# The seam of a first FFN and an attention: batch 0's output and norm into the last FFN units, batch 1's end, norm, keys and values into the first three head pairs

## What is computed

```python
x = x + 0.5 * ffn(layernorm(x))      # "first FFN"
x = x + attn(layernorm(x))
x = x + 0.5 * ffn(layernorm(x))      # same weights, "second FFN"

def ffn(h):       # 4 experts mixed per batch by a gate on the pooled tokens
    w = top-2 gate of relu(mean(h) @ Wg1 + bg1) @ Wg2 + bg2
    q, k, v = h @ (sum_e w_e W_e) + b          # 16 heads of 8
    out = softmax(q k^T / sqrt(8)) v
    return out @ Wo + bo

def attn(h):      # 16 query heads of 64, one key/value head, a null key
    q = h @ Wq / 8; kv = concat(null_kv, h @ Wkv)
    out = causal softmax(q kv^T) kv
    return out @ Wout
```

## Time and profile before

| | us |
|---|---|
| three runs, median (lowest to highest) | 1282.89 (1278.74 to 1284.65) |
| the profiled execution, own time | 1280.69 |
| its span | 1279.0 |
| busy in the span: PE, DVE, ACT, POOL | 1157.0, 1061.4, 941.1, 307.7 |
| end of the first FFN's last value products | 378.57 |
| first score tile of the attention | 399.83 |
| first maximum of pairs 0, 1, 2, 3 | 401.66, 437.00, 465.26, 493.26 |

### The profile page before, as it was taken

One profiled execution on the slowest core, in us unless ns is written; L12 is line 12 of the kernel. 1 busy time (PEld: TensorE's weight loads), 2 busy tenths in 40 slices (PEclk: granted clock), 3 DMA queues, 4 the chain that ended last, 5 costly groups with the idle time before them and its releaser, 6 DMA issues. The chain is left out here.

```text
span 1279.0 us, 31986 instructions
## 1 busy us (share of the span) xinstructions
PE 1157.0 (90%) x10884; PEld 502.0 (39%) x10884; DVE 1061.4 (83%) x1787; ACT 941.1 (74%) x2001; POOL 307.7 (24%) x535
## 2 busy tenths in 40 slices
PE   4499999998987899999999999998769999999996
PEld 3122222222225555555566565555522222222223
DVE  6899999998987777777755777776589999998997
ACT  3179999998983677777755777775339999998994
POOL 4400000022000354444432444443330000000200
PEclk9689999999997999999999999998869999999998
DMA  4812212354210001000000000000431212244422
GB/s 109 247 32 56 64 52 60 81 88 85 66 41 19 18 23 29 18 17 18 18 18 18 18 18 18 18 18 2 149 99 48 69 47 55 75 79 88 83 48 67
DMA packets 51793, 69.55 MB, mean 54 GB/s; under 512 B 21168, under 2 KB 29296, under 8 KB 51696
## 3 DMA queue, kind: packets, MB, share of 16 engines
q1 hardware_dynamic: 51696, 68.26, 21.7%
HBM read 37.30 MB, written 22.54 MB: 47 GB/s over the span
## 5 line engine op out<-in xcount | busy, mean ns | idle before, releaser
L959 DVE TENSOR_REDUCE neg_max<-ps 128x1 f32<-128x1024 f32 x512 | 594.5, 1213 | 26.6 <-PE ps L1230 22.8
L795 ACT ACTIVATE arena<-ps 128x512 f32<-128x512 f32 x1024 | 545.3, 597 | 84.2 <-PE ps L1245 71.9
L1261 PE MATMUL ps<-arena 128*32 128x256 f32 (+1 forms) x3584 | 317.1, 426 | 25.0 <-ACT arena L795 24.2
L1245 PE MATMUL ps<-arena 50*128 50x512 bf16 x1024 | 309.2, 388 | 6.2 <-DMA arena<-max_dram 5.6
L1230 PE MATMUL ps<-arena 48*128 48x512 bf16 x1024 | 282.6, 397 | 16.8 <-DVE neg_max L959 14.4
L1031 DVE TENSOR_REDUCE a_neg_max<-ps 128x1 f32<-128x129 f32 (+7 forms) x256 | 191.9, 750 | 110.4 <-PE ps L1382 109.4
L634 POOL TENSOR_SCALAR arena<-arena,a_rsum 128x128 f32<-128x128 f32 (+7 forms) x256 | 191.1, 747 | 310.8 <-DVE a_rsum L1050 303.5
L731 ACT ACTIVATE arena<-ps,a_neg_max 128x129 f32<-128x129 f32 (+7 forms) x256 | 189.2, 739 | 51.0 <-DVE a_neg_max L1031 38.5
L1377 PE MATMUL ps<-arena 64*128 64x128 f32 (+6 forms) x512 | 192.6, 457 | 0.0
L1375 PE MATMUL ps<-arena 64*128 64x321 f32 (+7 forms) x512 | 187.9, 450 | 4.9 <-DVE neg_s_null L1062 1.9
L1245 PEld LDWEIGHTS ps<-arena 50*128 50x128 bf16 x1024 | 71.7, 94 | 258.2 <-ACT arena L795 226.3
(11 more groups left out here) (125 smaller groups left out, 820.5 us busy)
## 6 DMA issues: line engine op xcount, KB each, us to landing
arena<-stack_dram SPq DMA_DIRECT2D x128, 192.0 KB, 3.4
stack_dram<-arena SPq DMA_DIRECT2D x48, 256.0 KB, 3.8
o_dram<-arena SPq DMA_DIRECT2D x32, 256.0 KB, 2.1
arena<-arena SPq DMA_DIRECT2D x32, 256.0 KB, 3.6
arena<-o_dram SPq DMA_DIRECT2D x30, 256.0 KB, 4.4
arena<-max_dram SPq DMA_DIRECT2D x256, 1.0 KB
x<-in_L_attn_x SPq DMA_DIRECT2D x2, 512.0 KB, 4.9
max_dram<-max_T SPq DMA_DIRECT2D x64, 8.0 KB, 1.7
```

The source lines that it names most:

```text
L795: nc.scalar.activation(probs[:, t, :], ps[:, EXP_BANK[t], :], ACT.Exp, scale=F_SCALE).then_inc(probs_ready, 1)
L959: nc.vector.tensor_reduce(neg_max[:, g, t:t + 1], ps[:, bank:bank + 2, :].rearrange("p a b -> p (a b)"), AX, ALU.max, negate=True).then_in ...
L1245: ins = nc.tensor.matmul(ps[:, bank, :], stack[rows, g, 1, kt * P:(kt + 1) * P], stack[rows, g, 0, h * HALF:(h + 1) * HALF], start=True, s ...
L1261: ins = nc.tensor.matmul(ps[row:row + 32, PV_BANK, cols], v_unit[:, g, t // 2, :], probs[:, t, cols], start=j == 0 and c0 == 0 and g % 2 == 0,
```

## The change

- Batch 0's product with Wo (`finish_0_half`) goes into the last two units: its halves ahead of score tiles (g, kt) = (2, 6) and (3, 1) of the last iteration, through banks 3 and 4. DVE's `finish` of batch 0 and its norm follow at once; ACT's square root stands after the exponential t = 8 of the last unit.
- POOL adds 0.5 * bo to all of x in the seventh of eight iterations of each FFN (`bias`), so `finish` needs one instruction for each half.
- `null_values` goes to the start of the first FFN, between the max tiles of unit 0 and those of unit 1; ACT copies it out after its splits.
- After the last unit PE has only the transposes, queries, keys, values and null scores of batch 0.
- Batch 1's sums, reciprocals and scaling are shared out: additions and scaling on POOL, `recip_1` on DVE (first half before the attention, second half in steps 1 and 3), `normalize_last` in step 6. Its products with Wo are four takes "Z" in steps 8 to 14 of pair 0, added by DVE's `add_quarter`.
- Batch 1's norm is in pair 1 (one `bn_stats` in each of steps 0 to 7, square root at ACT's step 9, reciprocal in step 11, the rest in steps 12 to 15); its transposes, keys, values and null scores are takes "N", "K", "A", "S" in steps 1, 2, 4, 6, 8, 10 of pair 2.
- PE's wait for batch 1's values is dropped from pairs 0 to 7.

```diff
+        SECOND_STEPS = {t: ("Z", t // 2 - 4, 0) for t in (8, 10, 12, 14)}
+        for t, take in ((1, ("N", 0, 0)), (2, ("N", 1, 0)), (4, ("K", 0, 0)), (6, ("K", 1, 0)), (8, ("A", 0, 0)), (10, ("S", 0, 0))):
+            SECOND_STEPS[2 * NS + t] = take
...
+                def bias():
...
+                    for b in range(B):
+                        pool.wait_ge(xn_ready, 4 * B * ph + 2 * b + 2)
+                        for g in range(2):
+                            xs = x[:, b * NT + 4 * g:b * NT + 4 * g + 4, :]
+                            nc.gpsimd.tensor_tensor(xs, xs, bo[:, :].unsqueeze(1).broadcast_to([P, 4, C]), ALU.add).then_inc(x_biased, 1)
...
+                if ph == 0:
+                    pool.wait_ge(o_loaded[1], 16 * (PAIRS_B - 1))
+                    r = slice(0, P - LR)
+                    for g in range(2):
+                        s = slice(g * HALF, (g + 1) * HALF)
+                        for kind, total in ((1, den), (0, num)):
+                            nc.gpsimd.tensor_tensor(total[r, 1, s], o_all[r, 1, 2 * g, kind, :], o_all[r, 1, 2 * g + 1, kind, :],
+                                                    ALU.add).then_inc(den1_ready, 1)
+                    pool.wait_ge(den1_ready, 4)
...
             def attention():
+                scale_1(0)
                 for t in range(NS):
                     normalize(0, t)
...
+                    if t == 5:
+                        scale_1(1)
...
+                    if s == 3:
+                        act.wait_ge(o_stored[1], 16 * (UNITS // NB) + 16)
+                    if s == NS + 9:
                         norm_std(B + 1, 1)
...
+                    if t == 8 and g == 3 and isinstance(it, int) and it == UNITS // NB - 1:
+                        norm_std(B, 0)
...
-                    nc.vector.tensor_tensor(ytmp[:, :, :].rearrange("p (a t) c -> p a t c", a=2), y,
-                                            bo[:, :].unsqueeze(1).unsqueeze(1).broadcast_to([P, 2, 2, C]),
-                                            ALU.add).then_inc(dve_link, 1)
...
+                nc.vector.scalar_tensor_tensor(xs, y, 0.5, xs, ALU.mult, ALU.add).then_inc(x_ready, 1)
...
+                    if s in (1, 3):
+                        recip_1(1, (s - 1) // 2 * (HALF // 2), (s + 1) // 2 * (HALF // 2))
+                    if s == 6:
+                        normalize_last(0)
...
+                    if 0 <= t < NT:
...
+                        ins = nc.vector.bn_stats(stats[:, NT + t, :], x[:, NT + t, :])
...
+                    if t == 11:
+                        dve.wait_ge(std_ready, B + 2)
+                        dve.wait_ge(xT_done, 2 * B + 2)
+                        link(nc.vector.reciprocal(rstd[:, NT:2 * NT], rstd[:, NT:2 * NT]))
...
+                    if isinstance(it, int) and it == UNITS // NB - 1 and (g, kt) in ((2, 6), (3, 1)):
+                        finish_0_half(0, g - 2)
                     score_tile(g, it, kt, 0)
...
+                for k in range(2):
+                    cols, tok = slice(k * C, (k + 1) * C), slice((2 * z + k) * P, (2 * z + k + 1) * P)
+                    nc.tensor.matmul(ps[:, bank, cols], num[0:P - LR, 1, tok], wo[0:P - LR, :], start=True, stop=False)
+                    ins = nc.tensor.matmul(ps[:, bank, cols], num_last[r, k * P:(k + 1) * P], wo_last[r, :], start=False, stop=True)
...
+                if ph == 0:
+                    null_values()
                 for t in range(NT):
                     max_tile(1, i0, t)
+                if ph == 0:
+                    pe.wait_ge(null_ready, 1)
```

More of the change, by code:

```diff
@@ L619, in body @@
                             null_weights()
+                        if isinstance(ul, int) and ul == (HB + 1) * NB and g == 2:
+                            bias()
                 body(0, False)
@@ L646, in attention @@
             def attention():
+                scale_1(0)
                 for t in range(NS):
                     normalize(0, t)
[L649 to L653, removed]
+                    if t == 5:
+                        scale_1(1)
+                for pg in range(1, 4):
+                    for t in range(NS):
+                        normalize(pg, t)
+                        if t in (1, 5) and pg % 2:
+                            add_null(pg // 2, t // 4)
+                with pool.Fori(4, B * PAIRS) as i:
                     for t in range(NS):
@@ L1150, in ffn @@
                     recip_0(ph, g)
-                for g in range(2):
-                    normalize_1(ph, g)
-                finish(ph * B, 0)
                 if ph == 0:
+                    finish(0, 0)
                     norm(B, 0)
-                normalize_last(ph)
-                if ph == 0:
+                    recip_1(0, 0, HALF)
                     for h in range(2):
@@ L1163, in ffn @@
                     values_in(0)
-                finish(ph * B + 1, 1)
+                    null_scores_in(0, Q_BANK)
+                else:
+                    for g in range(2):
+                        normalize_1(ph, g)
+                    finish(ph * B, 0)
+                    normalize_last(ph)
+                    finish(ph * B + 1, 1)
             ffn(0)
@@ L1310, in keys, with second_take @@
+            def second_take(kind, k):
+                if kind == "Z":
+                    out_take(k)
+                    return
+                wait_taken((kind, k, 0))
+                if kind == "N":
+                    norm_T_half(B + 1, k, TAKE_BANK["N", k, 0])
+                elif kind == "K":
+                    keys(1, k)
+                elif kind == "A":
+                    key_values(1)
+                else:
+                    null_scores(1, TAKE_BANK["S", 0, 0])
             def keys(b, h):
@@ L1549, in ffn @@
                     key_values(0)
-                finish_last(ph)
+                    pe.wait_ge(w_null_ready, 7)
+                    pe.wait_ge(probs_ready, TB + TB * UNITS)
+                    null_scores(0, Q_BANK)
+                else:
+                    finish_0(ph)
+                    finish_1(ph)
+                    finish_last(ph)
             ffn(0)
```

218 lines of the change are left out of this document (126 added, 92 removed).

## The result

| | before | after |
|---|---|---|
| median of 20 runs, us | 1282.17 | 1291.87 |
| lowest to highest | 1278.27 to 1285.92 | 1278.74 to 1297.91 |
| profiled execution, own time and span | 1280.69, 1279.0 | 1289.16, 1287.4 |
| ratio after / before, 95% interval | | 1.0058 (1.0038 to 1.0077) |

The change makes the kernel slower by 0.6%, where 2.6 us of gain were forecast; the median lies above the forecast range, which ended at 1288.0. The spread says more than the median: the runs of before lie within 8 us; those of after are in two groups, nine from 1278.7 to 1289.2 and eleven from 1291.7 to 1297.9. They go with the mean granted clock: the five quickest have 0.959 to 0.962, the eleven slowest 0.942 to 0.951.

The account below looks back on a forecast made before the run. PE bounds full pairs (27.38 of 28.00 us); the seam is a 21.3 us chain with little throughput work. Terms sum to -2.6 us, 1278.1 from the profiled 1280.7; with the median 2.2 higher, 1280.3 us; range 1272.5 to 1288.0.

Parts of the forecast that it names:

- Pair 0: First attention pair: root, null-score wait and value product leave, other work enters; 4.6 us shorter, 5.3 gained with first maximum.
- the takes Z: Batch 1's output products in pair 0: 3.75 us of PE at the lower clock, mostly in waits; 1.1 us lost.
- The clock: Last unit: the pause for the root may lower PE's clock; 1.0 us lost, between 0 and 4.0.
- B: Rival: moved work is paid again in full in pairs 1 and 2; total +5.2 us, 1288.1 us; chance 0.15.
- C: Rival: the clock falls in the last unit and stays down; 3.0 us more, 1283.3 us; chance 0.11.
- three signs of being wrong: Pair 0 stays at 35 us, pair 1 exceeds 33, or the last unit grows by more than 6 us.
- the null product: Start of the first FFN, between two max tiles: delays DVE's next maximum; 2.6 us lost, bounds 1.1 and 3.4.
- the chain from the values to the first score: Seam: batch 0's finish and norm leave it; values end at 383.0, first score at 392.5 instead of 399.8.
- pair 2: Third attention pair: batch 1's transposes, keys, values and null scores at PE's bound; 5.1 us lost, bounds 4 and 8.3.
- the inserted halves: Last unit: two insertions of batch 0's product on PE, 0.75 us each; 1.5 lost, bounds 0 and 2.1.
- the root with its clock: Last unit: ACT's root with two table loads, 2.9 us in full, and 1.0 for a fall of the clock.
- Pair 1: Second attention pair: DVE's added pieces cost 0.8 us, ACT's root 2.1; 2.7 lost, bounds 1 and 7.3.

Follow-up runs that it names:

- run 1: The changed kernel measured once more with no edit: median 1284.05 us, ratio 1.0039 to the kernel before.
- run 10: The changed kernel without the 16-row products of batch 1's output, two 112-row products a take: median 1282.46 us, ratio 0.9999 to the kernel before.
- run 5: The changed kernel with both moved norms' roots on DVE (linear guess, three Newton steps) instead of ACT: median 1285.08 us, ratio 1.0029 to the kernel before.
- run 8: Only the change's part inside the first FFN, roots on DVE, null product at the seam: median 1274.17 us, ratio 0.9951 to the kernel before.
- run 7: The changed kernel with output takes grouped, null product back at the seam, roots on DVE: median 1280.42 us, ratio 0.9990 to the kernel before.

## Why the prediction was wrong, point by point

| | forecast, us | first profile | run 1's profile |
|---|---|---|---|
| start of the first FFN | +2.6 | +2.8 | +2.8 |
| last unit, with the clock | +5.4 | +6.7 | +6.7 |
| values' end to first score | -11.7 | -12.1 | -11.9 |
| first score to first maximum | -0.7 | -1.2 | -1.2 |
| pair 0 | -4.6 | +7.6 | -2.4 |
| pair 1 | +2.7 | +4.1 | +4.2 |
| pair 2 | +5.1 | +5.4 | +5.5 |
| end of the attention (two levels) | 0 | -4.3 | -4.3 |
| end of the second FFN | -1.4 | -1.7 | -2.2 |
| all the rest | 0 | +1.1 | +2.6 |
| span | -2.6 | +8.4 | -0.2 |

The last column is no sign that the change costs nothing: at the level that the kernel before had at the end of the attention, the quick execution would be 4 us slower than it, and the first profile 13.

**The step that failed is "Pair 0"**, and in it the term of the takes Z: 3.75 us of PE at the lower clock, counted 1.1 on the path. That row had eight 112-row products in a line, and I left out the eight 16-row products that the takes also have, and the turns. The eight alone would have been 1.26 us by the row of `finish_last`; among the 112-row ones they cost as much as these. Measured, a take is 2.9 us at the lower level and 1.67 at the full one: 11.6 or 6.7 us. A block of 2.9 us inside a loop of two us a step isn't hidden by its waits. With half of the products gone (run 10) pair 0 is 31.1 us.

**The deeper fault is in "The clock".** I priced a fall of the clock in the last unit, at 1.0 us within 0 and 4.0, and none in pair 0, although before the clock was also down for a good part of it. It is this level that decides 10 us: 43.0 against 33.0 us of pair 0 in the same kernel. So no rival had the time of the measured median: B, the slowdown, gives 1288.1 by another mechanism, and C puts the clock in the wrong place. Of the three signs of being wrong that the prediction named, two came: pair 0 did not fall below 35 us (in the first profile), and the last unit grew by 6.7 us, more than 6; pair 1 stayed below 33.

The fall in the last unit was also read wrongly. The prediction took its pause of 2.3 us as hardly as long as the one in the earlier trace rows; but there PE's last product ends at 380.55, the clock is 1.00 up to 382.4 and 0.50 from 383.0, so 2.1 us of pause had been enough. In the kernel after it fell at 382.0, 1.3 us behind PE's last product (380.79).

**Right to within 0.6 us:** the null product (2.6, measured 2.8), the chain from the values to the first score (the 9.5 us behind the values were 9.2 and 9.3), pair 2 (5.1, measured 5.4; PE at its bound pays in full), and the end of the second FFN: from the last values to the last addition to x it was 14.2 us and is 12.4 and 11.9, so 1.7 or more against 1.4.

**Sizes off:** the inserted halves, 2.2 for 1.5 (just above the bound of 2.1), the root with its clock 4.5 for 3.9, that is 1.6 for the clock instead of 1.0 if the root is its 2.9. Pair 1: 4.1 for 2.7. Its table loads cost 1.8 or somewhat more (run 5), priced at 2.1, so the excess is in DVE's part: pair 1 without loads is 30.6 us, 2.6 above a full pair, where I had 0.8; the eleven instructions of the root on DVE are in the 2.6. Pieces of 0.2 to 0.5 us before a maximum are not hidden by its idle time as I had it; that is rival B's mechanism, at about half strength.

**The rules cited.** The drain of the Trainium skill (ScalarE: Activation LUTs, What ACT_TABLE_LOAD costs) is not in these rows: 379.71 to 381.01 is load and root, 381.33 the second load, 382.62 the next exponential. Two drains of 1.38 us would have been 2.8 us more, not the 2.4 of the prediction. The Trainium skill's page SBUF — State Buffer (on which operations take the shared pair) agrees in direction with the next rows: the first addition of normalize_last, beside POOL's normalization, took 0.76 us instead of the 0.42 of its twin; that makes 0.3 us, not the 2 of the estimate:

```profile
407.02 0.69 POOL L670 TENSOR_SCALAR arena<-arena,a_rsum 128x512 f32<-128x512 f32 x1 [0.30 <-POOL arena L670]
...
407.22 0.76 DVE L1040 TENSOR_TENSOR arena<-arena 128x256 f32<-128x256 f32 x1
...
408.02 0.42 DVE L1041 TENSOR_TENSOR arena<-arena 128x256 f32<-128x256 f32 x1
```

**Left open:** what in the turns keeps the clock down. The runs show that the slower group goes with them among kernels of like length (8 of 24 and 0 of 24 in one job), not what the chip reacts to; and run 8 has a slower group without them. Nor is it shown what sets the level at the end of the attention and in units 26 and 27. In run 7 the end of the attention accounts for 4.6 us of what the repairs lack in the profiles; what is left of the difference is open.

## What to carry to other kernels

Before moving work out of a stretch full of waits into stages that run at an engine's bound, price it there in full; here 9.6 us were paid in pairs 1 and 2 for a pair 0 that was 2.4 us shorter at best and 7.6 longer in the first profile. Price TensorE work at both levels of its clock wherever the granted clock dips, and count every product of the moved step, narrow ones too. Add the stages up to the whole span: what is left over is where nobody looked. A median hides a kernel with two levels: look at the spread of times beside the mean clock of each execution before looking for the cause in one trace.

## What the runs showed of the hardware

- With PE busy 23.8 of 23.8 us its clock stayed at 0.50 throughout; in another execution of the same kernel the same takes ran at 1.00. A busy share in a profile is no sign that the full clock is granted.
- The same 32 products behind the same wait took 8.49 us in one execution and 5.81 in another, in a stage that no kernel here changes.
- A float32 product with 128 columns and new weights took 0.72 us at the lower clock and 0.42 at the full one where 112-row and 16-row weights on the same partitions take turns, and about 0.58 and 0.32 in groups of two, whether of 112 or of 16 rows; eight of 112 rows in a line took 0.47 each at the lower clock. Eight of 16 rows in a line that goes over four groups of partitions took 0.16 and 0.09 each.
- In a pause of PE of 2.5 us in an otherwise dense stretch the clock fell (1.3 us behind PE's last product, and 0.51 from 382 to 389); with the two table loads that cost 4.5 us in the last unit. Without the pause it stayed at 1.00 (run 5).
